# Router scores of sequence 0 spread by TensorE for two experts, shared expert moved up, fill reordered

## The reference

```python
h = _layernorm(x, axis=-1) * (1 + ca) + sa
x = x + ga * attn(h)                       # scores, bias, softmax, values, wo
h = _layernorm(x, axis=-1) * (1 + cb) + sb
x = x + gb * ffn(h)
...
scores = softmax(xt @ gate_w.T)            # ffn: the router
top_scores, sel = jax.lax.top_k(scores, 2)
...
h = silu(xe @ w1[e]) * (xe @ w3[e])        # xe: the token times its score for expert e, or 0
out_routed = out_routed + h @ w2[e]
...
out = (silu(xt @ w1s[0]) * (xt @ w3s[0])) @ w2s[0] + out_routed
```

## Time and profile before

| | |
|---|---|
| Median of 3 runs | 665.83 us (665.41 to 667.18) |
| Profiled execution | 666.87 us, its span 664.9 us |
| TensorE busy (matmuls) | 644.2 us, 97% of the span |
| VectorE | 587.4 us, 88% |
| GpSimd | 579.5 us, 87% |
| ScalarE | 557.4 us, 84% |
| Granted clock of TensorE, mean | 0.993 of full |

### The profile page before, as it was taken

How to read it: one execution, slowest core, us unless ns; L and a number is a source line. 1 busy time by engine, 2 the same in 40 slices (tenths; PEclk the granted TensorE clock), 3 DMA queues, 4 the chain that set the end, 5 groups by cost and what they waited for, 6 DMA issues and landing times. The chain is left out here.

```text
span 664.9 us, 19607 instructions
## 1 busy us (share of the span) xinstructions
PE 644.2 (97%) x6136; PEld 563.2 (85%) x6136; DVE 587.4 (88%) x1582; ACT 557.4 (84%) x2458; POOL 579.5 (87%) x684
## 2 busy tenths in 40 slices
PE   8899989999999999999999999999999999999997
PEld 6888768888888898989898888888898888888776
DVE  5588868999999999999999999999999999997765
ACT  5598888989898999999898999999898998895442
POOL 7575767999999999999999999999999998888864
PEclk9899999999999999999999999999999999999999
DMA  6787777777877788777888797788778686805041
GB/s 219 194 217 158 211 211 207 207 206 206 240 196 199 191 237 212 209 201 223 221 208 205 184 244 196 206 229 219 204 202 229 176 237 170 238 13 162 3 149 33
DMA packets 194647, 127.51 MB, mean 192 GB/s; under 512 B 110784, under 2 KB 171632, under 8 KB 194416
## 3 DMA queue, kind: packets, MB, share of 16 engines
q1 hardware_dynamic: 194544, 126.27, 70.6%
HBM read 96.10 MB, written 30.14 MB: 190 GB/s over the span
## 5 line engine op out<-in xcount | busy, mean ns | idle before, releaser
L1244 ACT ACTIVATE p<-ps_s,nmx 128x96 f32<-128x96 f32 x1024 | 332.3, 347 | 28.9 <-DVE nmx L1793 27.6
L1244 ACT ACTIVATION_READ_ACCUMULATOR p<-ps_s,nmx 128x1 f32 x1024 | 218.1, 213 | 0.0
L766 POOL TENSOR_TENSOR xs<-h,sbc 128x512 f32<-128x512 f32 x128 | 166.1, 1306 | 5.3 <-DMA sbc<-s_scr 4.1
L772 POOL TENSOR_TENSOR xl<-xs,xh 128x512 fp32r<-128x512 f32 x120 | 154.0, 1285 | 16.4 <-ACT xh L1266 15.5
L2794 PEld LDWEIGHTS ps_s<-k,q 128*128 128x128 f32 x1024 | 139.6, 192 | 22.9 <-ACT p L1244 7.3
L1793 DVE TENSOR_REDUCE nmx<-ps_s 128x4 f32<-128x384 f32 x256 | 136.5, 547 | 25.3 <-PE ps_s L2794 23.4
L2861 PE MATMUL ps_Y<-w2s,g 128*128 128x128 f32 x1152 | 153.6, 279 | 1.3 <-DVE g L1911 1.3
L2861 PEld LDWEIGHTS ps_Y<-w2s,g 128*128 128x128 f32 x1152 | 140.2, 192 | 6.6 <-DVE g L1911 2.1
L2794 PE MATMUL ps_s<-k,q 128*128 128x96 f32 x1024 | 139.9, 269 | 5.6 <-DMA q<-q_scr 2.2
L1820 DVE STREAM_TRANSPOSE pt<-p 128x384 f32<-128x384 f32 x256 | 135.7, 558 | 1.7 <-POOL p L829 0.8
L1902 DVE SCALAR_TENSOR_TENSOR th<-th,ps_A 128x512 f32<-128x512 f32 x136 | 91.9, 676 | 10.1 <-ACT th L1287 8.8
(11 more groups left out here) (149 smaller groups left out, 1026.4 us busy)
## 6 DMA issues: line engine op xcount, KB each, us to landing
sbc<-s_scr SPq DMA_DIRECT2D x64, 512.0 KB, 6.2
k<-k_scr SPq DMA_DIRECT2D x62, 384.0 KB
q<-q_scr SPq DMA_DIRECT2D x128, 96.0 KB
k<-k_scr SPq DMA_DIRECT2D x31, 336.0 KB
k_scr<-kh SPq DMA_DIRECT2D x32, 256.0 KB, 3.1
q_scr<-qh SPq DMA_DIRECT2D x32, 256.0 KB, 2.9
xr<-x SPq DMA_DIRECT2D x16, 256.0 KB, 4.0
k_scr<-kl SPq DMA_DIRECT2D x16, 256.0 KB, 2.8
```

What stands on the lines that cost most here:

```text
L766: nc.gpsimd.tensor_tensor(xs[:, n % 2], h2[:, par], sbc[:, n - 1], ALU.mult).then_inc(xs_d, 1)
L772: nc.gpsimd.tensor_tensor(xl[:, n % XRING], src, xh[:, n % XRING].bitcast(F32), ALU.subtract).then_inc(xl_d, 1)
L1244: last = nc.scalar.activation(p[:, n % PRING, gg, :], ps_s[:, n % 2, MK * gg:MK * gg + MK], ACT.Exp, bias=nmx[:, n, gg:gg + 1], accum_out= ...
```

## The change

For sequence 0 the scores of experts 1 and 2 no longer go through memory. Two new steps `spread(0)`, `spread(1)` on TensorE multiply `smT` from the left with single columns of the identity, repeated 128 times, which puts one expert's scores on all partitions in bank A or B; two new steps `take_scores` on ScalarE copy the banks into `sbc`. `get_scores(0, 0)` goes; `get_scores(0, 1..3)` and `put_scores(0)` stay. The shared expert of sequence 0 (`expert(0, 0)`, its tanh, `half_silu`, `combine`, `down`) moves to an earlier place in all lists. Beside that the fill's lists of all five engines are reordered at many places, and TensorE's fillers go from 182 to 146. `body` and `drain` are as before, but that the semaphore counts of `get_scores` are shifted by one for experts 1 and 2.

```diff
+        def scores_in(b, k):
+            return 16 * b + (0 if k == 0 else 16)
...
 put_scores(b)                                     # SyncE
-                        sp.wait_ge(s_in[k], 16 * b)
+                        if k > 0 or b > 1:
+                            sp.wait_ge(s_in[k], scores_in(b - 1, k))
+                    if b == 1:
+                        sp.wait_ge(sb_d, 2)
...
 fill                                              # SyncE
                 load_k(2, 0, 0)
-                load_ga(2)
                 put_scores(0)
-                get_scores(0, 0)
                 get_scores(0, 1)
...
                 load_k(2, 1, 0)
-                load_x(4)
+                load_gb(0)
+                load_ga(2)
                 load_bias(4)
                 put_q(3, 1)
                 put_ql(3, 1)
+                load_x(4)
...
 scaled(b, n, par)                                 # GpSimd
-                if n % 2 == 1:
-                    pool.wait_ge(s_in[n // 2], 16 * b + 16)
+                if seq_is(b, 0) and n <= 2:
+                    pool.wait_ge(sb_d, n)
+                elif n % 2 == 1:
+                    pool.wait_ge(s_in[n // 2], scores_in(b, n // 2))
...
+            def take_scores(e):                   # ScalarE
+                act.wait_ge(sp_mm, e + 1)
+                act.wait_ge(s_wl, 2)
+                act.wait_ge(s_w2, 1)
+                nc.scalar.activation(sbc[:, e], ps["AB"[e]][:], ACT.Copy).then_inc(sb_d, 1)
...
+            def spread(e):                        # TensorE
+                pe.wait_ge(smt_cp, 1)
+                if e == 0:
+                    pe.wait_ge(v_d, 1)
+                else:
+                    pe.wait_ge(g_d, 1)
+                for a in range(NQB):
+                    row = NQB * e + a
+                    last = mm(ps["AB"[e]][:, QB * a:QB * a + QB],
+                              ident[0:NQB * NE, row:row + 1].to_broadcast([NQB * NE, 128]), smT[:], start=True, stop=True)
+                last.then_inc(sp_mm, 1)
...
 fill                                              # VectorE
-                maximum(1, 12)
                 route_sum(0)
                 route_inverse(0)
-                maximum(1, 13)
+                turn_p(1, 8)
+                turn_p(1, 9)
+                turn_p(1, 10)
                 route_top(0)
+                maximum(1, 12)
                 route_which(0)
+                maximum(1, 13)
                 route_index(0)
                 route_select(0)
-                turn_p(1, 10)
+                half_silu(0, 0, 0)
+                combine(0, 0, 0)
...
 fill                                              # TensorE
                 scores(1, 11)
+                router(0, 0)
                 values(1, 0)
                 values(1, 1)
                 values(1, 2)
-                router(0, 0)
                 values(1, 3)
+                expert(0, 0)
+                scores(1, 12)
+                scores(1, 13)
+                scores(1, 14)
                 values(1, 4)
```

More of the change, by code:

```diff
@@ L489, in fill @@
                 load_k(1, 1, 1)
+                load_ga(1)
                 load_bias(3)
-                load_ga(1)
-                load_gb(0)
                 load_x(3)
@@ L964, in fill @@
                 scaled(2, 5, 0)
+                gate_wo(4)
                 expand_v(4, 1)
@@ L2877, in expert @@
                     pe.wait_ge(v_d, bank_user(b, n))
+                if n == 1 and first:
+                    pe.wait_ge(sb_d, 2)
                 exact3(bank_a, w13h[:, e, 0, :], w13l[:, e, 0, :], xh[:, n % XRING], xl[:, n % XRING]).then_inc(a_mm, 1)
@@ L2945, in fill @@
                 values(0, 10)
-                warm(8)
+                warm(4)
+                values(0, 11)
+                warm(5)
                 scores(1, 0)
@@ L2961, in fill @@
                 scores(1, 5)
-                warm(5)
+                attn_out(0)
+                warm(3)
                 scores(1, 6)
-                attn_out(0)
                 project_q(2)
@@ L3006, in fill @@
                 values(1, 11)
+                scores(2, 3)
+                scores(2, 4)
+                down(0, 0, 0)
                 values(1, 12)
                 values(1, 13)
-                warm(2)
                 values(1, 14)
                 values(1, 15)
-                scores(2, 3)
-                scores(2, 4)
-                expert(0, 0)
-                project_q(3)
                 scores(2, 5)
@@ L3021, in fill @@
                 expert(0, 2)
-                down(0, 0, 0)
                 project_k(3)
+                values(2, 0)
+                values(2, 1)
+                values(2, 2)
+                values(2, 3)
                 scores(2, 8)
@@ L3051, in fill @@
                 values(2, 9)
-                values(2, 10)
+                down(0, 4, 0)
                 expert(0, 6)
@@ L3059, in fill @@
                 expert(0, 7)
+                scores(3, 2)
+                values(2, 10)
                 values(2, 11)
```

209 lines of the change are left out of this document (97 added, 112 removed).

## The result

| | before | after |
|---|---|---|
| Median of 20 runs each, side by side | 666.19 us | 668.89 us |
| Ratio, 95% interval | | 1.0033 [1.0019, 1.0046] |
| Profiled execution (span) | 666.87 us (664.9) | 668.77 us (666.9) |
| Granted clock, mean over the span | 0.993 | 0.982 |

The forecast was 662.3 us with a range of 660.0 to 665.4.

A forecast was written before the change was run, and what follows sets the result against it. TensorE, saturated from about 104 to 600 us, was taken to bound the kernel. One broadcast less (2.1 us) plus the moved expert (1.4) made 3.5 us, so 662.3 us against a median of 665.83; 8-in-10 range 660.0 to 665.4.

The forecast's parts named there:

- What bounds the kernel: TensorE, saturated from about 104 to 600 us: only letting it reach that part earlier moves the end, one for one.
- The early part, 0.4 us earlier: Reordered lists, 16 to 60 us: net 0 to 0.7 us earlier, 0.4 taken, used up by router_t.
- Rival 2: Without 26 fillers the clock falls earlier; scores(2, 0) about 2.5 us late, 1 us of gain left, 664.8 us; chance 0.10.
- One broadcast less, 2.1 us: SyncE, sequence 0: get_sums(1) issued at 92.1 instead of 94.19, so o and attn_out(1) come 2.1 us earlier, at 96.4.
- The spread, 2.1 us: Both spreads on TensorE ahead of scores(2, 0) take 2.1 us together, replacing fillers and a 0.83 us wait: no loss.
- router_t unchanged at 80.1: Routing of sequence 0: sel 0.6 us earlier, but router_t still at 80.1; bounds 0.8 earlier, 1.0 later.
- The moved expert, 1.4 us: expert(0, 0) and down(0, 0) leave the stretch around attn_out(1): 1.4 us gained behind it, bounds 0.4 and 2.5.

The follow-up runs named there:

- five pairs: Pairs of kernels differing only in the early part (TensorE's list up to scores(1, 5)), new against old order; mean ratio difference 0.0027, or 1.8 us.
- e1: Changed kernel with 11 filler matmuls put back between scores(1, 12) and spread(0); 667.51 us, ratio 1.0021 to the kernel before.
- e2: Kernel before without its 26 fillers between scores(1, 11) and scores(2, 2); 665.37 us, ratio 0.9994 to the kernel before.
- e15: The kernel before, unchanged, timed against itself under another label; 667.46 us, ratio 1.0027.
- e10: Changed kernel with TensorE's early part in the old order, the other four engines' new; 667.01 us, ratio 1.0023 to the kernel before.
- e7: Changed kernel with the early part in the old order and 11 fillers put back in the handover; 666.15 us, ratio 0.9999 to the kernel before.
- e13: Kernel before with only the handover (router of sequence 0 to router_t(1)) in the new order, spread and 11 fillers included; 665.85 us, ratio 0.9995.
- e5: Kernel before with the spread alone, early part and shared expert in their old places; 665.13 us, ratio 1.0005 to the kernel before.
- e16: Changed kernel with TensorE's early part in the old order, the same program measured a second time; 666.87 us, ratio 1.0019 to the kernel before.

## Why the prediction was wrong

- **What bounds the kernel** was right: the saturated part and the body are the same, and what counts is when TensorE gets there.
- **The early part, 0.4 us earlier**, is the step that failed most. It costs 1.8 us by the five pairs. I had read one wait in it that goes (0.69 us on ScalarE, not on TensorE) and one that comes, and priced the order by these two. The start comes 0.3 us earlier on average (`scores(0, 0)` at 26.4 against 26.7 us over seven and ten profiles, each anywhere from 25.6 to 27.5), and that is lost again by `scores(1, 0)`, which comes 0.5 us later on average. The other 1.3 us I can't place.
- **The clock.** Rival 2 named what happened, at 0.10. The 26 fillers went, and the clock fell at 79.8 us in the changed kernel and at 78.9 in its repeat, right behind the hole of 1.12 us at `scores(1, 14)`. Its price was off as well: it left 1 us of gain, since it expected most of the loss to vanish in the wait at `attn_out(1)`. In the profile that wait did shrink from 1.71 to 0.33 us, but `turn_sums(1)` moved with TensorE and carried `put_sums(1)` and `get_sums(1)` along. I had treated the transfer's issue as SyncE's affair alone. What it costs at the end is the estimate of 1.0 us from above. (The Trainium skill, "TensorE: Matmul & The Clock Gate", "Part 1", speaks for this rival: its clock follows how busy TensorE was of late. The runs agree on average, with 23.3 us of low clock without the fillers and 12.8 with them in e1, 22.8 and 9.8 in e2 and e15. A single execution is not settled by it: e10, with no fillers there and the same hole of 1.13 us, kept the full clock throughout the handover.)
- **One broadcast less, 2.1 us.** The issue came as forecast where nothing delayed it (92.31 in e7, 91.6 in e13, 92.3 in e5). The step from the issue to `o`, taken as a constant 3.5 us, was the mistake: it was 5.7 in e7 and 5.1 in e13, though 3.5 in e5 and e10. Measured, 0.8 us instead of 2.1. In the changed kernel itself the issue came at 95.55, 3.5 us after the forecast, since the sums were turned late.
- **The spread, 2.1 us**, was right at full clock (2.2 in e10), and in place of waiting and fillers cost nothing visible: from `router_t(0)` to `scores(2, 0)` it is 3.0 us in e7 and e13, against 3.2 before. At the low clock of the changed kernel it was 4.7.
- **router_t unchanged at 80.1** was 1.8 us off in the changed kernel. About 1 us of that is the early part in that profile (`scores(1, 0)` at 55.77 instead of 54.70). The rest lies between `scores(1, 0)` and `router_t(0)`, 26.1 us instead of 25.4. The kernels with the new handover take 25.3 to 26.0 there where the clock is full, so what part the low clock has in it and what part the six matmuls of the expert is open.
- **The moved expert, 1.4 us.** From `attn_out(1)` to `router(1)` the first profile of the kernel before took 11.22 us, its repeat, without the low clock there, 10.25. The new handover takes 9.4 to 10.7, mostly 9.6. So the 1.4 us was there against that one profile (11.22 to 9.6), but about 1 us of it was a low clock that belonged to that execution and not to the kernel; that the term came near its forecast is luck. Against the repeat 0.65 us are left, and 0.7 are given back in the beat to `turn_sums(4)`.

In sum: the handover's gains, 0.8 + 0.65 - 0.7 = 0.75 us, are about what a measurement here can't tell from nothing, and e7 and e13 show nothing. The early part adds 1.8 us and the clock, by the estimate, 1.0. That makes 2.0 to 2.8 us of loss; measured are 2.2 (0.0033) and 2.9 (0.0043). Two of these terms come from ratios of many runs and the three of the handover from single profiles, so that the agreement is no proof. Shown is that the early part costs time; where in it, and what the low clock costs, is not.

None of the kernels in the table beats the kernel before by more than the scatter.

## What to carry to other kernels

When a change takes a wait away in one place and moves the work that filled another, price both together: here the shared expert was what hid a transfer, and the new path only paid for its move. A transfer that is issued earlier need not land earlier; read its time to landing beside what the DMA engines still carry. Fillers on TensorE could be taken out at no cost where TensorE waits anyway (e2); where real work on its path follows at once, measure it before you do. A gain read from one profile should be checked in a second profile of the same kernel before it is booked.

## What the runs showed of the hardware

- The low clock comes or not in one and the same program: e10 had none from 80 to 99 us, e16 13.7 us of it from 81.5 us on, with the same two holes just before on TensorE, 0.35 and 1.13 us in e10, 0.33 and 1.13 in e16.
- Four fp32 products out of 32 rows (x8 in the row, as each is recorded twice) take 1.15 and 1.05 us at full clock, as four of `down` out of 128 rows do, 1.06. (The Trainium skill, "TensorE: Matmul & The Clock Gate", "Why this matters for your kernels", says that a contraction of 32 takes as long as one of 128; the trace agrees.)
- The kernel before, timed against itself, came out 0.27% slower [0.07, 0.46], though both were timed side by side on one chip. Run by run the times of the kernel before scatter by 1.5 us (standard deviation of 152 runs). What sets a whole series off by 1.8 us was not found.
